# Depthwise filters of a two-layer network on 32x32 tiles of TensorE: a group's four filters in one step

## What is computed

```python
def _causal_dw_conv(x_bcl, w_ck):          # per channel, K taps
    K = w_ck.shape[-1]
    return conv_general_dilated(x_bcl, w_ck[:, None, :], window_strides=(1,),
                                padding=[(K - 1, 0)], feature_group_count=x_bcl.shape[1])
...
paths = [_fir(v_direct, f) for f in (fir_w3, fir_w7, fir_w15, fir_w31)] + [delta_out]
router_in = concatenate([hidden_states] + [p.reshape(B, L, H * DV) for p in paths], axis=-1)
hmid = gelu(router_in @ router_W1 + router_b1)
probs = softmax((hmid @ router_W2 + router_b2).reshape(B, L, H, 5) / tau[:, None])
ctx = sum(probs[..., i:i + 1] * paths[i] for i in range(5))
o = context_mass[..., None] * ctx + p_value_adj[..., None] * v_direct
```

## Time and profile before

| | us |
|---|---|
| time, median of 3 runs | 1002.55 |
| lowest, highest | 1002.01, 1006.68 |
| span of the profiled execution | 1004.1 |
| PE busy | 932.3 (93%) |
| DVE busy | 742.6 (74%) |
| ACT busy | 650.3 (65%) |
| POOL busy | 334.5 (33%) |

### The profile page before, as it was taken

The page is one execution under the profiler, slowest core; times in us unless marked ns, Lnnn a source line. Parts: engine busy times, 40 slices in busy tenths (PEclk is TensorE's granted clock), DMA queues, the critical chain, the costliest instruction groups (busy, mean ns, idle before and its releaser), DMA issues.

```text
span 1004.1 us, 22014 instructions
## 1 busy us (share of the span) xinstructions
PE 932.3 (93%) x7958; PEld 593.9 (59%) x7958; DVE 742.6 (74%) x2882; ACT 650.3 (65%) x1474; POOL 334.5 (33%) x720
## 2 busy tenths in 40 slices
PE   6988899999986989999999999999977899999996
PEld 3877574644433556677876656665334555677674
DVE  3556789899899986866374797869999996665514
ACT  5699899866442236679898867765432356787653
POOL 4765342625022012736243331141340022342232
PEclk7999999999987799999999999999986999999998
DMA  9400002030453120100000000223443200000001
GB/s 308 175 2 1 1 1 52 2 83 14 95 128 75 43 70 17 44 22 12 1 12 1 11 11 1 53 60 94 90 97 76 57 21 22 2 11 1 12 1 32
DMA packets 77692, 45.44 MB, mean 45 GB/s; under 512 B 53008, under 2 KB 68880, under 8 KB 77328
## 3 DMA queue, kind: packets, MB, share of 16 engines
q1 hardware_dynamic: 77584, 44.04, 16.5%
HBM read 33.01 MB, written 11.01 MB: 44 GB/s over the span
## 4 chain that ended last, share of the span: by engine, by line
PE 57%; DVE 27%; ACT 8%; POOL 4%; issue 3%; DMA 0%; SPq 0%; POOLq 0%; ACTq 0%; DVEq 0%
PE psum L1101 7%; DVE pool L1588 5%; DVE sol_t L1593 5%; PE psum L558 5%; PE psum L1091 4%; PE psum L859 4%; PE psum L833 3%; PE psum L831 3%; PE psum L994 3%; DVE pool L1531 3%; PE psum L920 3%; PE psum L1085 2%; PE psum L1087 2%; ACT pool L1823 2%; PE psum L567 2%
## 5 line engine op out<-in xcount | busy, mean ns | idle before, releaser
L1809 ACT ACTIVATE pool<-psum 128x512 f32<-128x512 f32 x144 | 84.0, 595 | 64.4 <-PE psum L558 22.4
L2185 POOL TENSOR_SCALAR small<-small 128x4 f32<-128x4 f32 x88 | 22.2, 252 | 283.6 <-DVE small L1173 281.4
L1823 ACT ACTIVATE pool<-pool,small 128x128 f32<-128x128 f32 x224 | 91.5, 486 | 27.3 <-POOL small L2190 27.1
L558 PE MATMUL psum<-sb_const,pool 128*128 128x128 f32 x672 | 100.9, 283 | 6.4 <-ACT pool L1823 2.9
L920 PE MATMUL psum<-pool,firw 128*32 128x512 f32 (+7 forms) x960 | 103.2, 571 | 0.0
L558 PEld LDWEIGHTS psum<-sb_const,pool 128*128 128x128 f32 x672 | 79.3, 145 | 37.9 <-issue 22.3
L2188 POOL TENSOR_TENSOR small<-small,minus_half 128x4 f32<-128x4 f32 x88 | 92.2, 1048 | 7.3
L994 PE MATMUL psum<-pool,sb_l1a 128*128 128x512 f32 x192 | 88.6, 612 | 0.0
L1101 PEld LDWEIGHTS psum<-sb_l1f,pool 128*128 128x128 f32 x640 | 77.2, 192 | 11.3 <-issue 9.5
L1101 PE MATMUL psum<-sb_l1f,pool 128*128 128x128 f32 x640 | 82.8, 278 | 0.0
L1404 DVE TENSOR_TENSOR pool<-pool,psum 128x512 f32<-128x512 f32 x80 | 52.4, 682 | 37.8 <-ACT pool L2095 16.2
(11 more groups left out here) (429 smaller groups left out, 2139.5 us busy)
## 6 DMA issues: line engine op xcount, KB each, us to landing
pool<-scratch_kk SPq DMA_DIRECT2D x18, 256.0 KB, 3.8
pool<-in_cF SPq DMA_DIRECT2D x16, 256.0 KB, 3.1
scratch_kk<-pool SPq DMA_DIRECT2D x10, 256.0 KB, 2.6
pool<-in_xF SPq DMA_DIRECT2D x8, 256.0 KB, 6.2
pool<-in_x SPq DMA_DIRECT2D x8, 256.0 KB, 7.0
scratch_xt<-pool SPq DMA_DIRECT2D x8, 256.0 KB, 2.0
pool<-scratch_xt SPq DMA_DIRECT2D x8, 256.0 KB, 3.2
scratch_kk<-pool SPq DMA_DIRECT2D x32, 64.0 KB, 1.9
```

The costliest lines, as they stand in the source:

```text
L558: m = e.transpose(f.ap[:, part(b)], src[:, part(b)], ident)
L1809: e.activation(slot(g, i), f.ap, ACT.Copy).then_inc(f.emptied, 1)
L1823: m = e.activation(dst[:, part(b)], src[:, part(b)], ACT.Identity, bias=v["nm"][:, b:b + 1], scale=v["r"][:, b:b + 1])
```

## The change

The four filters of a group become one step, on tiles of 32 rows and 32 columns. SBUF partitions of the shifted values now run over 32 r + 4 u + s (head r, channel u of 8, shift s of 4), and slot 8 + c holds the channels 8 c + u of each head. One tile (r, c) takes eight channels with four shifts (32 rows of weights) to eight channels of all four filters (32 columns). A group takes eight rounds (NKG = 8) of 16 matmuls; the row tile is the outer loop and the column tile the inner one. Head r fills bank r, so a group's step takes four banks at once and ACT copies them one after another.

```diff
         def b_fir(g, k):
             o.wait_ge(made, MADE["s_b2"])
-            o.wait_ge(sem("edge_zeroed"), 3 * g + 3)
-            o.wait_ge(sem(f"shifted{g % NA}"), 64 * (g // NA + 1))
-            f = begin("b_fir", g, "s", k)
+            o.wait_ge(sem("edge_zeroed"), g + 1)
+            heads_f = [begin("b_fir", g, f"h{r}") for r in range(4)]
             vsh = slot(g, 8, 4).rearrange("p (c b t) -> p c b t", c=4, b=GB)
-            kgs = [kg for ff, kg in FIR_GROUPS if ff == k]
-            for n, kg in enumerate(kgs):
-                for c in range(4):
-                    col = FIR_GROUPS.index((k, kg)) * 4 + c
-                    m = e.matmul(b4(f.ap)[32 * c:32 * c + 32, :, 4 * kg:], firw[:, col, :],
-                                 vsh[:, c, :, 0:P - 4 * kg], start=n == 0, stop=n == len(kgs) - 1)
-            m.then_inc(f.filled, 1)
+            for kg in range(NKG):
+                for r in range(4):
+                    r_ = slice(32 * r, 32 * r + 32)
+                    for c in range(4):
+                        m = e.matmul(b4(heads_f[r].ap)[32 * c:32 * c + 32, :, 4 * kg:], firw[r_, kg, c, :],
+                                     vsh[r_, c, :, 0:P - 4 * kg], start=kg == 0, stop=kg == NKG - 1)
+                    if kg == NKG - 1:
+                        m.then_inc(heads_f[r].filled, 1)
```

```diff
+        def s_w(g, k):                       # TensorE
+            landed(o, "const", "once_l1")
+            f = begin("s_w", g)
+            ...
+            o.wait_ge(sem("rows_by_shift"), 1)
+            for c in range(4):
+                for r in range(4):
+                    m = e.matmul(f.ap[32 * r:32 * r + 32, nfg * c:nfg * c + nfg], pick[:, c, :], fir[:, :, r], start=True, stop=True)
+            m.then_inc(f.filled, 1)
```

`b_sh` writes the values with four DMAs in place of one, to reorder the rows, and waits for all four; the four shifted reads go to every fourth partition. `b_ez` becomes one POOL instruction:

```diff
-            for s in range(1, 4):
-                settle()
-                e.memset(vsh[32 * s:32 * s + 32, :, :, 0:s], 0.0).then_inc(*mark("edge_zeroed", 3 * g + s))
+            e.tensor_tensor(cells, cells, shift_col[:, 0:3].unsqueeze(1).to_broadcast([P, NP, 3]), ALU.mult).then_inc(
+                *mark("edge_zeroed", g + 1))
```

The router's weights of the four filter paths are loaded in the new row order, by 16 small DMAs (18 for l1a in place of one, ahead of the load of l0f). ACT's `b_fir` is now four copies in a row:

```diff
-            evacuate("b_fir", g, 3 + k, k)
+            for r in range(4):
+                f = full("b_fir", g, f"h{r}")
+                e.activation(slot(g, 3 + r), f.ap, ACT.Copy).then_inc(f.emptied, 1)
```

More of the change, by code:

```diff
@@ L51 @@
[L51 to L60, removed]
@@ new lines @@
+g_out/2 b_q/6 b_fir/4 f_e.0/7 b_kk/4 b_ag/4 b_sol/4 f_e.1-3/7 b_k/6 b_ks/5 b_k2/5 f_hid.5/7 f_e.4-5/7 b_qs/5 b_q2/5
+b_v/6 f_d.0-2/7 b_vs/6 f_d.3/7 b_ks/6 f_d.4/7 b_ez/5 f_d.5/7 f_out/7 b_x.0-3/4 b_ss/5 b_x.4-5/4 b_k2/6 b_qs/6 b_x.6-7/4
+b_sh/6 b_ez/6 b_qn/5 b_x.8-9/4 g_na/3 g_out/3 b_x.10-31/4 b_gg/5 b_x.32-41/4 b_vT/5 b_x.42-44/4 b_q2/6 f_na/7 b_fir/5
+b_kk/5 b_x.45-52/4 b_ag/5 b_x.53-58/4 b_vT/6 b_x.59/4 b_ss/6 b_x.60-61/4 b_xo/4 b_tr/7 b_q/7 b_k/7 b_qs/7 b_v/7 b_vs/7
+b_sol/5 b_x.0-1/5 b_qn/6 b_x.2-3/5 b_gg/6 b_x.4-6/5 b_ks/7 b_k2/7 b_x.7-20/5 b_fir/6 b_rs/4 b_xt/4 b_x.21/5 b_rl/4
@@ L132 @@
+g_out/7
 """
@@ L166 @@
 }
-for _name in ("b_kk", "b_at"):
+for _name in ("b_kk", "b_at", "b_fir"):
     BANKS[_name, 0] = [(f"h{_k}", (_name, 0)) for _k in range(NH)]
@@ L374, in landed @@
         for p_ in parts:
-            own.wait_ge(sem("ld_" + p_), 16)
+            own.wait_ge(sem("ld_" + p_), 16 * (18 if p_ == "l1a" else 1))
     CHUNKED = {"diagonals": 4, "triangles": 6, "inverses": 8, "turned": 12}
@@ L527, in sync @@
         a_load(EARLY[1], 0)
-        for p_ in ("l1a", "l0f"):
-            load(p_)
+        rw1 = cols["l1a"]["rw1"][0]
+        load("l1a", 0, rw1 + 256)
+        load("l1a", rw1 + 5 * 256)
+        for c in range(4):
+            for f in range(4):
+                src = dram["l1a"][:, rw1 + (1 + f) * 256:rw1 + (2 + f) * 256].rearrange("(j c u) m -> c u j m", j=4, c=4)[c]
+                dst = wt("l1a", "rw1", 256, 1024).rearrange("p (j m) -> p j m", j=4)
+                e.dma_start(dst[32 * c + 8 * f:32 * c + 8 * f + 8], src).then_inc(sem("ld_l1a"), 16)
+        load("l0f")
         for g in EARLY:
@@ L989, in b_r @@
         def b_r(g, k):
-            got("b_fir", g, "s", 3)
+            got("b_fir", g, "h3")
             got("b_oF", g)
@@ L1137, in g_b7 @@
             m.then_inc(f.filled, 1)
-        steps = dict(s_a=s_a, s_x=s_x, s_b1=s_b1, s_y=s_y, s_g1=s_g1, s_g2=s_g2, s_g3=s_g3,
+        steps = dict(s_a=s_a, s_x=s_x, s_b1=s_b1, s_w=s_w, s_y=s_y, s_g1=s_g1, s_g2=s_g2, s_g3=s_g3,
                      a_y=a_y, a_s0=a_s0, a_km=a_km, a_kt=a_kt, a_ga=a_ga, a_err=a_err, a_dots=a_dots, a_c=a_c, a_s1=a_s1, a_out=a_out,
@@ L1784, in g_st @@
             stats("g_st", g, slot(g, 0))
-        steps = dict(s_a=s_a, s_m=s_m, s_x=s_x, s_f=s_f, s_b1=s_b1, s_b2=s_b2, s_y=s_y, s_g1=s_g1, s_g2=s_g2, s_g3=s_g3,
+        steps = dict(s_a=s_a, s_m=s_m, s_x=s_x, s_f=s_f, s_b1=s_b1, s_w=s_w, s_b2=s_b2, s_y=s_y, s_g1=s_g1, s_g2=s_g2, s_g3=s_g3,
                      a_s0=a_s0, a_ga=a_ga, a_kt=a_kt, a_err=a_err, a_c=a_c, a_out=a_out,
```

254 lines of the change are left out of this document (150 added, 104 removed).

## The result

The change makes the kernel slower: 1021.46 us (median of 4 runs, 1020.68 to 1021.96) against 1004.62 us of the kernel before in the same series; the ratio is 1.0163, with a 95% interval of 1.0138 to 1.0187. The forecast was 1003 us. The profiled execution spans 1020.2 us against 1004.1.

A forecast was written before the change was run, and what follows sets the result against it. It took PE, 93% busy, as bound in some stages and DVE in others; 1.3 + 0.4 + 2.1 + 0.3 − 0.7 − 0.3 − 2.5 = +0.6 us on 1002.55 gave about 1003 us, range 995 to 1012.

The forecast's parts named there:

- the clock: PE's granted clock, 0.56 from 247 to 254 us: less PE work may start, lengthen or move this; booked 0, ±4 us.
- The block: Group's 16-tile filter step: about 6.3 us for 12.9, tiles at once; +0.1 us in each of three chain blocks, +0.3.
- rival D: Filter blocks: the tiles don't work at once, blocks on the chain grow; 1022 us, or 1013 at 9.5 us a block; chance 0.10.
- lies under DVE: Filters of groups 2, 3, 5, 6 and 7: what they save on PE is hidden by DVE's work; no gain.
- The banks: Four banks filled at once, emptied by ACT alone: +2.1 us at group 1, +0.4 at group 0, group 4 covered.
- Groups 4 to 7: 655 to 695 us: DVE's wait for L1101 nearly vanishes, the output DMA wait takes part back; −2.5 us, groups 5 to 7 nothing.
- groups 0 to 3: Filters before about 330 us: −0.7 us between 188 and 265 us, nothing from group 0 or from groups 2 and 3.
- SP's loads: Start: 17 more load issues on SP take 7 to 13 us; booked nothing, up to 7 us if they came last.
- the edge step: Three short memsets against one short product on POOL, done well ahead of the filters; stays hidden.
- the mix: DVE's additions of filter results: a group gains or loses 0.3 us, mostly under PE; booked −0.3 once, bounds ±2.5.
- the setup: New weight step `s_w` and DVE work at the start make PE go on later; booked +1.3 us, from 0 to 2.5.
- Rival C: Bank emptying and clock drops on the path: 2 x 2.4 us and 3 us more, 1011 us; chance 0.18.

The follow-up runs named there:

- the control: The changed kernel run again as the same program, with nothing edited; ratio to the kernel before 1.0171.
- e4: The kernel before with the three shorter filters left out, each one matmul of 16 columns, all else as before; ratio 1.0074.
- e9: The changed kernel plus the shorter filters' work as filler steps at their old places, with a bank each and results nobody reads; ratio 1.0130.
- e19: The changed kernel with the filler steps and the output DMA of group 2 issued ahead of group 5's shift step; ratio 1.0148.
- e6: The changed kernel with ACT's four copies of a block in the order of heads 3, 2, 1, 0; ratio 1.0238.
- e12: The changed kernel with each of ACT's four copies cut to 32 of 512 columns; ratio 1.0129.
- e17: The changed kernel with filler steps, copies cut to 32 columns, four filter rounds for eight, and group 2's output DMA issued ahead of group 5's shift step; ratio 1.0076.

## Why the prediction was wrong

**The step that failed is the price of work that PE is spared: the clock.** "I book 0, with ±4", it said, and priced in everything else a microsecond that PE is spared at nothing or at a gain. Spared work isn't free here. The shorter filters stood where PE would otherwise wait for DVE, ACT or POOL, and they kept its clock up. Without them the clock falls at 187, 238, 269, 286 and 682 us (in the control at four of these places, not at 269), and what runs slow then is in part on the path. e4 shows this in a kernel without any other part of the change (+0.74%, lag 3.2); the filler shows the way back (2.9 to 5.7 us of the lag, over e9, e19 and both executions of the changed kernel). In the first half the filler gives back 2.2 to 5.0 us, where the missing work alone cost about 1, so it may cost more beside the longer blocks than without them; no run tells these apart. I had read the one low stretch of the kernel before and its cause, and should have asked at each removed filter what PE would do in its place. By its size this step alone doesn't make the miss: 10 us stay with the filler. The terms of the block, of the banks and of groups 4 to 7 failed beside it, and how the 14 to 16 us split among them isn't told exactly, since the gains of the experiments don't add up.

**The block: a term of +0.3 us that is +4.8 for the three blocks alone.** The 16 tiles run at once (rival D as such is refuted), but I took the pace from the columns, and a round takes about 0.2 us more. The upper bound of my range, 37 ns a record from the row tiles, was nearer than the 14 ns that I took: it is 31 ns. The three blocks that were on the chain are 1.6 us longer each, and those of groups 2, 3 and 7 joined it (of the "two short pieces" that I read, one was 5.1 us long already). So "lies under DVE" held for what they save and not for what they cost. The Trainium skill's 10.6-fold speedup (TensorE: Matmul & The Clock Gate, Part 3) gave an estimate of 9.6 us; measured are 7.94, between it and my 6.3.

**The banks: right in kind, too small.** PE's wait for group 1 is there, 1.28 us where I worked out 2.1. But short copies take 4.4 to 6.5 us off in all, against 2.5 booked; e6 shows how many steps want these banks. I counted two places. The Trainium skill's warning (TensorEngine Tiling (Array Packing), Performance Considerations), that emptying PSUM may become the bottleneck, is borne out by e12.

**Groups 4 to 7: −2.5 booked, about +5.5 measured** (5.4 in the control). The lag did fall by 5.5 us at 672 us, DVE's wait for L1101 is gone, and the wait for the output DMA did take its place. But e17 shows that this wait wasn't the cap, at least where filler, short copies and half rounds are there too: without it, 3.6 of 4.4 us are lost all the same.

**What held:** nothing gained in groups 0 to 3; SP's loads, the edge step and the mix free, and no sign that the shift step costs; the setup, booked at +1.3 with 0 to 2.5, measured at 2.0 and 2.5. Rival C had the right mechanism, at 1011 us for two banks and one clock drop; there were four or five drops, and longer blocks besides.

**What stays open:** about 4 us at group 4 that remain when filler, short copies, half rounds and an early DMA are all there, and some 2 to 3 us behind 700 us in most variants. A clock drop and a wait on DVE are seen there, but no run took them away. What makes the 0.2 us of a round, and whether the holes come from the instruction queue, wasn't tried either. And the lag is known from one execution of each edit, so effects under 2 us aren't told apart.

## What to carry to other kernels

Work that PE did here while it would otherwise have waited cost nothing and earned something: before taking such work out, look up at its place what PE waits for next, and count the clock behind that wait as a price. Price a block of packed tiles from a block of the same tiling, not from its columns: here each round took 0.2 us more than those, and one of the rows at hand, 37 ns a record, came nearer than the columns did. When a block grows longer, look for blocks beside the chain that will join it. A step that fills four banks at once needs someone who empties them at once; find every step that is dealt one of them, not just the next.

## What the runs showed of the hardware

A kernel with some 50 us less work for TensorE was 0.74% slower. The changed kernel with as much idle work added back ended 10.1 and 10.8 us behind in the profile, without it 13.7 and 15.8. 32x32 matmuls of 400 to 512 columns on all 16 tiles came at 31 ns a record with the clock at 1.00, and of 200 to 256 columns at 20 to 23 ns, with holes between; a round of 16 tiles took its columns and about 0.2 us. The 18 holes of more than 0.5 us each ended 1.0 to 1.6 us after a packet on the instruction queue had landed. Two executions of one program differed in where the clock fell, by up to 3.6 us at one place and 2.1 us at the end.
